# Second attention's start: weights issued beside the last expert tiles, norms a piece ahead, and first work before the branch

## The reference

```python
x = x + _L0_gnn_ref(_layernorm(x), adj, L0_gnn_W, L0_gnn_r)
x = x + _L0_ffn_ref((_layernorm(x))[None], gate_w, gate_b, W1, b1, W2, b2)[0]
x = x + _L1_gnn_ref(_layernorm(x), adj, weight, weight_u, weight_v, bias, proj_w, proj_b)
x = x + _L1_ffn_ref((_layernorm(x))[None], Wr, br, ln_g, ln_b, W1, b1, W2, b2)[0]

def _L1_gnn_ref(inputs, adj_mat, weight, weight_u, weight_v, bias, proj_w, proj_b):
    N, IN_F, H, D = (4096, 256, 4, 64)
    support = (inputs @ weight).reshape(-1, H, D).transpose(1, 0, 2)
    f1 = jnp.einsum('hnd,hd->hn', support, weight_u[..., 0])[:, None, :]
    f2 = jnp.einsum('hnd,hd->hn', support, weight_v[..., 0])[:, :, None]
    scores = jax.nn.leaky_relu(f1 + f2, 0.2)
    # masked with adj, softmax over axis 2 (max, exp, sum), then:
    out = jnp.einsum('hnm,hmd->hnd', attn, support)
    out = out.transpose(1, 0, 2).reshape(-1, H * D) + bias
    return out + inputs @ proj_w.T + proj_b
```

## Time and profile before

| | us |
|---|---|
| median of 3 runs | 1848.31 (1845.47 to 1851.26) |
| profiled execution, device time | 1845.97 |
| its span, first to last instruction | 1844.2 |
| PE busy in the span | 1675.1 (91%) |
| DVE busy | 929.3 (50%) |
| ACT busy | 955.2 (52%) |
| POOL busy | 350.6 (19%) |

### The profile page before, as it was taken

The page is one execution under the profiler, slowest core; times in us unless marked ns, Lnnn a source line. Parts: engine busy times, 40 slices in busy tenths (PEclk is TensorE's granted clock), DMA queues, the critical chain, the costliest instruction groups (busy, mean ns, idle before and its releaser), DMA issues.

```text
span 1844.2 us, 41619 instructions
## 1 busy us (share of the span) xinstructions
PE 1675.1 (91%) x13344; PEld 1547.9 (84%) x13345; DVE 929.3 (50%) x2185; ACT 955.2 (52%) x2192; POOL 350.6 (19%) x315
## 2 busy tenths in 40 slices
PE   4799999999799994767989989989988999999998
PEld 3588888778799994657989979989987999999997
DVE  4578877888322222338877868867773111111111
ACT  1143443543434432347989979979834443443443
POOL 2110000000266663210000000000001333333332
PEclk9899999999899997788999999999998999999999
DMA  9990000005388886200000000000094666666664
GB/s 159 107 164 10 9 9 17 29 18 200 114 208 206 207 212 174 80 14 7 17 15 13 14 13 18 9 18 18 3 332 157 178 189 174 179 190 173 181 187 94
DMA packets 85581, 189.95 MB, mean 103 GB/s; under 512 B 13209, under 2 KB 59545, under 8 KB 76665
## 3 DMA queue, kind: packets, MB, share of 16 engines
q1 hardware_dynamic: 51801, 138.33, 22.9%
q0 software_dynamic: 31504, 48.97, 16.7%
q10 hardware_dynamic: 2192, 1.58, 0.3%
HBM read 188.98 MB, written 33.11 MB: 120 GB/s over the span
## 4 chain that ended last, share of the span: by engine, by line
PE 51%; DVE 4%; DMA 2%; ACT 2%; issue 2%; ACTq 0%; DVEq 0%; POOL 0%; SPq 0%; POOLq 0%
PE bank L1625 23%; PE bank L2107 12%; PE bank L2146 11%; PE bank L619 1%; PE bank L616 1%; DMA arena<-proj_b 1%; ACT arena L1376 1%; PE bank L2114 1%; DMA arena<-qd 1%; DVE arena L1469 0%; DVE arena L1471 0%; PE bank L2036 0%; PE bank L2010 0%; PE bank L606 0%; DVE arena L1413 0%
## 5 line engine op out<-in xcount | busy, mean ns | idle before, releaser
L1625 PE MATMUL bank<-arena 128*128 128x195 bf16 x5408 | 475.9, 250 | 43.3 <-DVE arena L1471 35.7
L1625 PEld LDWEIGHTS bank<-arena 128*128 128x128 fp8e4 x5408 | 470.8, 98 | 48.5 <-issue 46.5
L1376 ACT ACTIVATE arena<-arena,m_row 128x512 fp8e5<-128x512 f32 (+1 forms) x672 | 401.6, 678 | 68.6 <-DVE arena L1471 46.0
L2107 PEld LDWEIGHTS bank<-X,arena 128*128 128x128 f32 x2832 | 337.0, 194 | 8.7 <-issue 2.6
L2107 PE MATMUL bank<-X,arena 128*128 128x128 f32 x2832 | 339.2, 277 | 0.1
L2210 DVE TENSOR_TENSOR arena<-bank,X 128x256 f32<-128x256 f32 x118 | 50.1, 425 | 562.3 <-PE bank L2146 508.9
L2146 PE MATMUL bank<-arena,X 128*128 x1416 | 325.0, 379 | 2.2 <-ACT X L2184 2.1
L1245 PE MATMUL bank<-arena 128*128 (+1 forms) x1352 | 312.1, 386 | 15.1 <-DVE arena L1151 15.0
L1245 PEld LDWEIGHTS bank<-arena 128*128 128x128 f32 x1352 | 252.5, 191 | 55.7 <-issue 20.9
L2146 PEld LDWEIGHTS bank<-arena,X 128*128 128x128 f32 x1416 | 259.9, 190 | 33.2 <-issue 2.6
L1103 ACT ACTIVATE bank<-arena,s_all 128x384 f32<-128x384 f32 (+1 forms) x234 | 133.7, 573 | 185.5 <-DVE arena L1143 182.9
(11 more groups left out here) (235 smaller groups left out, 1341.2 us busy)
## 6 DMA issues: line engine op xcount, KB each, us to landing
arena<-m1w SPq DMA_DIRECT2D x67, 1024.0 KB, 10.6
arena<-m0w SPq DMA_DIRECT2D x67, 512.0 KB, 6.9
xs<-X SPq DMA_DIRECT2D x4, 1664.0 KB, 7.0
arena<-qd SPq DMA_DIRECT2D x25, 256.0 KB, 3.3
arena<-adjT POOLq DMA_DIRECT2D x13, 448.0 KB, 12.7
arena<-adjT POOLq DMA_DIRECT2D x13, 384.0 KB, 10.8
xe<-zeros POOLq DMA_DIRECT2D x1, 3456.0 KB, 21.7
X<-x_in SPq DMA_DIRECT2D x2, 1664.0 KB, 11.3
```

Source lines behind the costliest of these rows:

```text
L1376: last = a.activation(self.sign[slot].bitcast(F8W)[:, q * W:q * W + nt * P], self.row[r][:, 0:nt * P], ACT.Sigmoid, scale=STEEP, bias=self ...
L1625: last = pe.matmul(bank[rb * NT + n][:, kind * KW:(kind + 1) * KW], self.split[slot][kind].bitcast(F8)[:, q * W + n * P:q * W + (n + 1) * ...
L2107: last = pe.matmul(bank[2 * s + c // 4][:, c % 4 * P:(c % 4 + 1) * P], self.W1[s][:, k * HID + c * P:k * HID + (c + 1) * P], self.rxt[s][: ...
```

## The change

- **Weights.** A class `SecondWeights` gives the second attention's weights places in the arena that are free during the last expert tiles of layer 1, and one semaphore. `tiles_sync` issues their eight transfers on SP (among them the gate's two) right behind the last tile's load, before the barrier. ACT's six transfers and SP's two in the third block go.
- **Pieces.** `PIECES` is now 2, 3, 4, 4 pairs. DVE copies the attention vectors first, then takes the statistics of the whole next piece with a keep between, two to three pairs behind; the keep of a pair stands behind the norm of the piece that is due.
- **Before the branch.** DVE's row quantities, interleaved with the decision, and the first group of parts; ACT's exponentials, the steep copy, and one sigmoid that brings its table; SP's first row load. `own_row_tensor` stands ahead of `reach_tensor`. What the other side of the branch needs in addition (`far_begin_...`) is only there.
- `row_sync` is unrolled over the heads, with the same transfers in the same order.

```diff
@@ class SecondWeights
+            def load_sync(self, sp):
+                nw = 4 * L1.HD
+                sp.dma_start(self.wT..., w1T...).then_inc(self.loaded, 16)
+                sp.dma_start(self.wmat...[:, :, 0:nw], w1...).then_inc(self.loaded, 16)
...
+            ALL = 8 * 16
@@ tiles_sync
                 load_w1(RUN_TILES - 1, 0)
+                if behind is not None:
+                    behind(sp)
@@ class Attention
-            PIECES = (0, 3, 6, 9, PAIRS)
+            PIECES = (0, 2, 5, 9, PAIRS)
@@ pieces_vector
-                for j in range(self.PIECES[1]):
-                    add_stats(j)
-                norm_of(0)
                 v.wait_ge(self.wvec_ready, 1)
+                v.tensor_copy(gate_bias, second.gate_bias)
                 v.tensor_copy(gate, bank[4][:, 64:64 + KC * E])
...
-                for c in range(4):
-                    here, ahead = range(self.PIECES[c], self.PIECES[c + 1]), 0
-                    if c < 3:
-                        ahead = self.PIECES[c + 2] - self.PIECES[c + 1]
-                    for n, i in enumerate(here):
+                v.wait_ge(self.pb, 1)
+                v.memset(V.rearrange("p (c n) -> p c n", n=65)[:, :, 64:65], 1.0)
+                pieces = self.PIECES
+                for j in range(pieces[1]):
+                    add_stats(j)
+                norm_of(0)
+                kept = 0
+                for c in range(1, 4):
+                    for j in range(pieces[c], pieces[c + 1]):
+                        add_stats(j)
+                        if kept < pieces[c] - 2:
+                            for s in range(2):
+                                keep(kept, s)
+                            kept += 1
+                    norm_of(c)
+                    while kept < pieces[c] - 1 or (c == 3 and kept < PAIRS):
                         for s in range(2):
-                            keep(i, s)
-                        if c < 3 and n < 2:
-                            for j in range((0, 2)[n], (2, ahead)[n]):
-                                add_stats(self.PIECES[c + 1] + j)
-                            if n == 1:
-                                norm_of(c + 1)
+                            keep(kept, s)
+                        kept += 1
@@ class Signed
+            def first_row_sync(self, sp):
+                H = self.H
+                sp.wait_ge(self.A.own_stored, 16)
+                sp.wait_ge(self.row_used[0], 1)
+                sp.dma_start(self.row[0], qd...).then_inc(self.row_loaded[0], 16)
+            def early_scalar(self, a):
+                H = self.H
+                for s in range(2):
+                    a.wait_ge(self.A.vp_free[s], PAIRS + 1)
+                a.activation(d_all[:, 0:H * T], s_all[:, 0:H * T], ACT.Exp, scale=SLOPE)
+                a.activation(self.exp_sj[:, 0:H * T], s_all[:, 0:H * T], ACT.Exp).then_inc(self.exp_ready, 1)
+                a.activation(self.steep_sj, s_all[:, 0:H * T], ACT.Copy, scale=STEEP).then_inc(self.steep_ready, 1)
+                a.wait_ge(self.row_steps, H + 3)
+                a.activation(q_cols[:, 0:2 * H * T], q_cols[:, 0:2 * H * T], ACT.Exp).then_inc(self.exp_ready, 1)
+                a.activation(rden[:, 0:1], s_all[:, 0:1], ACT.Sigmoid)
+            def early_vector(self, v):
...
+                v.tensor_scalar(is_far[:, :], far[:, :], QUICK_REACH, None, ALU.is_ge).then_inc(A.far_known, 1)
+                v.wait_ge(self.exp_ready, 1)
+                self.scale_group(v, 0, 0, 4)
+                v.wait_ge(A.far_known, 1)
@@ blocks
-                X0.tiles_sync(sp, m0w1, m0b1, m0b2)
+                X0.tiles_sync(sp, m0w1, m0b1, m0b2, second.load_sync)
...
-                A1.back_load(sp, 0, 0, 1)
-                A1.gate_sync(sp, gate1, gate_b1)
-                A1.back_load(sp, 0, 1, 4)
+                A1.back_load(sp, 0, 0, 4)
...
+                Q1.first_row_sync(sp)
                 sp.wait_ge(A1.far_known, 1)
...
-                A1.far_vector(v)
+                Q1.early_vector(v)
...
-                A1.values_sync(a)
                 A1.pieces_scalar(a)
                 A1.own_row_scalar(a)
+                Q1.early_scalar(a)
...
-                A1.reach_tensor(pe)
                 A1.own_row_tensor(pe)
+                A1.reach_tensor(pe)
```

More of the change, by code:

```diff
@@ L486, in pieces_gpsimd @@
             def pieces_gpsimd(self, pool):
[L487 to L488 removed]
+                pool.wait_ge(self.w_loaded, second.ALL)
+                pool.tensor_tensor(self.pbias[:, 0:D], self.pbias[:, 0:D], second.proj_b, ALU.add
                                    ).then_inc(self.pb, 1)
```

168 lines of the change are left out of this document (102 added, 66 removed).

## The result

The changed kernel takes 1819.9 us (median; 1817.7 to 1822.4) against 1847.2 us for the kernel before beside it (1845.5 to 1851.3). The ratio is 0.985, with a 95% interval of 0.9835 to 0.9870: it is faster by 27.2 us (24.0 to 30.5). The forecast was 1824.0, the range 1818 to 1833. The profiled execution took 1817.7 us, with a span of 1815.9 us against 1844.2.

What follows compares the result with a forecast made beforehand. Bounds were late weights, three norm waits, half clock behind them, and branch supply gaps. Gains 11.5 + 9.5 + 3.7 - 0.4 = 24.3 us gave 1821.7 against the profiled 1845.97; the median forecast was 1824.0 us, range 1818 to 1833.

Steps and rivals of the forecast that it cites:

- the four terms: Gains from the third block's start to the first attention products: 11.5, 9.5 and 3.7 us, less 0.4 us for moved transfers.
- Weights ahead, first piece smaller: Third block's start: weights there at the barrier and `xe` landing 1.05 us earlier bring PE's first turn forward, gain 11.5 us.
- Late `xd`: Rival at the block's start: piece 1's `xd` half still lands at 744.3, time 1830.0; chance 0.12.
- Norms a piece ahead: Loop of 13 pairs: three norm waits and slow pairs (13.8 us) become three keep waits (4.3 us), gain 9.5 us.
- Clock falls in the new waits: Rival in the loop of pairs: PE loses full clock in the new waits, price 5.7 us, time 1829.7; chance 0.16.
- In front of the branch: DVE from the reach to the first split step: 9.0 us instead of 12.73, gain 3.7 us, between 1.9 and 4.
- The second gap: DVE's 1.77 us instruction supply gap behind the branch was to be hidden; rival that it stays: 1825.8, no separate chance.
- the margin of the signs: First split step: the signs were to be there near 827, 2 us before DVE needs them.
- The moved transfers: Layer 1's last expert tiles: weight loads sharing DMA engines with POOL's scatters cost 0.4 us, bounds 0 and 3 us.
- The unrolled loop "costs nothing": SP's row loads in `row_sync`: unrolling costs nothing because the transfers are the same.
- Slower than before: Rival in the long phase of products: clock keeps falling back, 600 further slow products would give 1857; chance 0.02.

## Why the prediction held, and where it didn't

- **The sum.** 24.3 us were forecast for the stretch, 24.0 are in the trace. That it is so close is luck in part: the four terms were off by +0.8, -0.5, +0.9 and -1.5 us. The median moved by 27.2 us (24.0 to 30.5), more than the stretch; in the profiles the changed kernel's rest is 4.2 us shorter too. That was in no term of mine.
- **Weights ahead, first piece smaller.** Right in mechanism: vectors under the load of `x`, then `xe` as the one that ends the start. It gave 12.3 us from the barrier, 0.8 more than taken. The mis-sized number is the landing of `xe`: 7.6 us after its issue for 9.5, 1.9 us earlier where I had 1.05 from the queue's rate. The norm of two pairs took 4.5 us, as taken. Undoing this part made the kernel 10 to 11 us slower by the ratios, against 14.5 - 1.7 us in the traces; that run had all eight transfers on one queue, so neither number is the part's worth over the kernel before.
- **Late `xd`.** Ruled out: 7.2 us to landing instead of 19.7, and DVE never waited for it. Without the transfers ahead of it, SP's queue had moved about 1.2 of the 1.3 MB of its first two pieces before POOL's queue sent its first packets, near 730. The Trainium skill, "DMA: Bandwidth & Descriptors", section on queues, rings and completion order, lets a DMA engine go round its queues packet by packet. The 80 and 80 packets agree. What that costs depended here on the time at which each queue started.
- **Norms a piece ahead.** Right: three waits for DVE's keep, 1.55, 1.56 and 1.56 us (forecast 1.4), clock 1.00 behind each. The loop gained 9.0 us for 9.5; the waits are 4.7 us together where I had 4.3, which is most of the difference.
- **Clock falls in the new waits.** It didn't, in any of the six waits of the two profiles of this kernel, nor in twelve more of 1.55 us in four other kernels. The kernel with waits of 2.5 us shows that the rival was near: 1 us more in each of them brings the half clock back in two of three.
- **In front of the branch.** 4.6 us for 3.7. The sum had the reading of the flag (0.72) ahead of the gap (3.00); measured is 3.17 us from the end of the parts to the split, so the flag's reading isn't on the path any more. Decision and rows took 1.67 us for 2.0. The second gap stayed away, and the kernel with this part undone has it back: what decides is what stands behind the landing. But the margin of the signs was mis-sized: I put it at 2 us, and it is 1.2 (the fourth sign ends at 807.2, the split starts at 808.40). The signs came when I had them, 6.9 us after the reach for 7.2; DVE was 0.9 us earlier. With the gap gone DVE waited 1.98 us for them. The Trainium skill, "Runtime: NRT & Kernel Launch", on instruction fetch, has a stall where the target is outside the fetched pages. The near landing agrees, with 0.16 us from the branch to its target.
- **The moved transfers.** This is the step that failed: I took 0.4 us, and it is 1.9. I had argued over order within one queue and over bytes, while the cost came at the scatters: DVE waited 4.24 us for one at 713.61, POOL issued the last one 1.7 us later after PE's last product than before, and all kernels without transfers behind the last tile begin the block 9.55 to 9.82 us after the last product, against 11.3 to 12.0. It was inside the bounds of 0 and 3 us. My own sign of being wrong here, a barrier later than 724, came: the block begins at 724.94.
- **The unrolled loop "costs nothing".** It gives: 0.45 us less of SP at each of three changes of heads, and a ratio of 0.9980 whose interval, up to 0.9996, just leaves out 1.
- **Slower than before.** Nothing of it: the first block of products has its old length, 30.6 us.

## What to carry to other kernels

Take loads from the head of a stage into the tail of the stage before, but look at three prices: bytes beside scatters that end that stage, issue time and bytes on the queue that feeds its loop (eight in a row cost 4 us here, one per pair of tiles nothing beyond the spread), and what becomes late next. When a wait is shortened, ask which wait takes its place and whether it is short enough to keep PE's clock; here 1.55 us kept it each time and 2.2 us lost it each time. A supply gap behind a branch is worth only what isn't hidden under it, and moved to the head of a dense stage it can cost the clock behind it, which was dearer here than the gap itself.

## What the runs showed of the hardware

- **A branch with a far landing** cost DVE 2.8 to 3.5 us from the branch to the target in these profiles (3.00 before, 3.04 in the changed kernel). Where short instructions stand behind the landing, a second gap of 1.5 to 2.1 us followed, which ended 2.8 to 3.1 us after the first of them had started; with longer ones it isn't seen. With a near landing, and longer instructions behind it, there is 0.16 us. At the end of the products the jump over the other side came with 5.25 us of idle time.
- **Waits and the clock.** Waits of 1.55 us kept the full clock 18 times of 18. Waits of 2.2 us (six) and 3.6 us (three) all lost it, in the kernel before and with the old pieces. Waits of 2.5 us kept it once and lost it twice, in one execution, under the same loop. A wait of 2.35 us at the head of the second routing lost it for over 20 us.
- **Addresses worked out in a loop** put 0.45 us on SP between the release and the transfer that follows it.
- **A row of 256 KB** took 3.15 to 3.48 us or 4.14 to 4.55 us at the same place of the same loop in the thirteen profiles with the unrolled loop, and nothing in between. What decides is open.
- **Loads beside scatters.** 1.06 MB of loads issued behind the last tile's load made the last scatter 1.6 to 2.3 us later after PE's last product, in seven profiles of seven.
